# A routed two-layer block on one core: down weights kept in freed memory, powers moved ahead of scatters, tails spread over three engines

## The chip, the cores and the metric

The kernel runs on one core of one Trainium2 chip. The core has five engines that run side by side: TensorE (PE, matrix products), VectorE (DVE), ScalarE (ACT), GpSimd (POOL) and SyncE (SP), which here starts DMAs. The metric is the device time of one execution in microseconds. Of the kernel before, three executions took 945.34, 945.8 and 950.18 us; the median is 945.8 us.

## The reference

The input is x with T = 2048 rows of D = 256 numbers. Four sublayers follow, each on a layer norm of x and added to x:

```
x = x + attn_a(layernorm(x))  # projections q, k, v (causal convolution, 4 taps), gate g; per head a
                              # recurrence: state = rotate(state)*alpha + beta*rotate(v)
                              # out * rsqrt(mean(out^2) + eps) * rms_w * silu(g), then @ Wo
x = x + ffn(layernorm(x))     # 8 experts, top 2 of softmax(h @ router), weights normed:
                              # y = silu(h @ gate) * (h @ up) @ down, summed over both experts
x = x + attn_b(layernorm(x))  # 16 heads of 16, window 128 and 16 persistent keys
x = x + ffn(layernorm(x))     # the same weights as the first ffn
```

The layer norm is (x - mean) / sqrt(var + 1e-5). All arithmetic is float32 in kind.

## The kernel before

Rows lie on the 128 partitions: 16 blocks of 128 tokens, in four groups of four blocks. The program is four stages, one after the other, with a barrier between them.

**Recurrence** (function `recurrence`, the profile's 0 to 277 us). A loop over four chunks of 512 tokens, `it` = 0 to 3. In each, TensorE sums squares per head (L398), VectorE stores them plus eps as `ms` (L713), GpSimd raises them to the power -1/2 (L587), TensorE transposes the result (L408), VectorE splits it (`rms_split`, L718) and scales the output, TensorE projects it back (L428), and VectorE adds it to x and takes statistics (`tail_stats_dve`). `tail_pool` (L154, L156) turns the variance into rstd on GpSimd. During chunk `it` the routing of group `it - 1` is worked out too: logits on TensorE, ranks and slots on VectorE. GpSimd then scatters the group's rows to the DRAM tensor `xs`, sorted by expert: eight indirect DMAs per group (`pool_scatter`, L1096), which wait for the last routing step (`shares`, L1029). On GpSimd's queue the scatters of group `it - 1` stand after `tail_pool` of chunk `it`, and so ahead of the power of chunk `it + 1`.

**Experts** (function `experts`, called twice, L1249 and around). A loop over 39 tiles of 128 sorted rows, in software pipeline steps. SyncE reads each tile from `xs` into `xin` (L1176, ring of four). TensorE transposes it (L1233), multiplies by gate and up (L1249), transposes the hidden values (L1259) and multiplies by the down weights `wd` (L1271). ScalarE copies and scales (L1309, L1316, L1324), VectorE makes products and copies (L1369, L1376) and the target rows (`aim`). GpSimd sends results to `back` in DRAM (L1211), and between them scatters the last group. SyncE issues the reads of the first two tiles, then the read of `wd` (L1193, 2 x 968 KB), then the other tiles. The same queue carries both.

After the tiles comes a tail, four groups of 512 tokens. SyncE reads two blocks of `back` per group, one for each expert (L1187, 512 KB each); two groups fit in memory, so group 2 waits until group 0 has been added. VectorE adds both (`mix`, L1383), takes statistics (L1389, L1393), normalises (L1399) and, after TensorE's transposes (L1282) and ScalarE's copy (L1329), splits off the low part (L1404). GpSimd does the power only. In the second call there is no norm: each group is stored to `out` instead.

**Attention** (function `attention`). Sixteen blocks in software pipeline: period `n` (0 to 19), five steps `u` in each. The tables `LOGITS`, `RANKS`, `RATIOS` and `SEND` name the steps (n, u) at which the routing of groups 0, 1 and 2 and their scatters stand. `max_rows` on SyncE moves the negated row maxima of a block (L1651). `keep` on GpSimd masks the probabilities (L1697, L1699), `rstd_of` does the power of a block's norm (L1688, L1691).

The order on each engine is the order in which the code is written; there is no scheduler. An engine waits at the head of its queue for semaphores.

## Time and profile before

| | us |
|---|---|
| median of three runs | 945.8 |
| the profiled execution | 952.93 |
| its span, first to last instruction | 951.1 |

| engine | busy us | share |
|---|---|---|
| PE, matmuls | 696.6 | 73% |
| DVE | 524.9 | 55% |
| ACT | 285.5 | 30% |
| POOL | 284.7 | 30% |

The mean granted TensorE clock is 0.764 of full speed. Of the 951.1 us the recurrence takes the first 277, the first experts stage runs to 448, attention to 799, the second experts stage to the end. In the profile a bracket after an instruction gives the time that its engine sat idle before it and what ended the wait; idle time counts only where others wait for that engine.

### The profile page before, as it was taken

To read this page: it belongs to the slowest core of one execution; us is meant where nothing else is said; L and a number is where in the kernel's file an instruction comes from. 1 tells how busy PE (TensorE), PEld (TensorE's weight loads), DVE (VectorE), ACT (ScalarE), POOL (GpSimd) and SP (SyncE) were. 2 spreads that over 40 slices of the span, in tenths; PEclk is the share of its full clock that TensorE was granted. 3 is DMA by queue.
4 is the path that set the end of the run, shared out by engine and by line. 5 is a ranking of instruction groups with operands and counts; after the bars stand their busy time and mean duration, and the time that the engine had idled before them with its cause. 6 is when DMAs were issued, how large, how long until landed. Compare 5 with 4: busy or idle time off the path is not lost. (4 is left out here: it accounts for less than half of the span.)

```text
span 951.1 us, 14101 instructions
## 1 busy us (share of the span) xinstructions
PE 696.6 (73%) x4483; PEld 546.2 (57%) x4483; DVE 524.9 (55%) x1373; ACT 285.5 (30%) x518; POOL 284.7 (30%) x345
## 2 busy tenths in 40 slices
PE   2857898866246899912368999998898986689980
PEld 1636676645234577701246787786786764457760
DVE  6493889768533444447444565466656354344434
ACT  1342332331001344401113443433432331224440
POOL 0001111312430544322501333323533553154340
PEclk9887897956565999955556897777965665789995
DMA  7897000100024333251643255145140003333328
GB/s 221 289 351 232 1 1 1 44 4 12 36 67 112 120 112 95 84 178 35 86 56 55 26 68 68 21 50 72 35 73 13 26 19 102 99 111 115 99 84 265
DMA packets 67915, 84.01 MB, mean 88 GB/s; under 512 B 8758, under 2 KB 62659, under 8 KB 67237
## 3 DMA queue, kind: packets, MB, share of 16 engines
q1 hardware_dynamic: 61028, 64.93, 29.3%
q0 software_dynamic: 6816, 18.19, 5.4%
q8 instruction: 39, 0.64, 0.3%
q14 instruction: 32, 0.25, 0.1%
HBM read 32.26 MB, written 39.06 MB: 75 GB/s over the span
## 5 line engine op out<-in xcount | busy, mean ns | idle before, releaser
L1211 POOL DMA_INDIRECT back<-f_yout,f_target x78 | 76.8, 984 | 163.8 <-ACT f_yout L1324 151.7
L1249 PE MATMUL bank<-f_wgu,f_xt 128*128 x312 | 116.0, 497 | 12.5 <-ACT f_xt L1309 10.9
L1369 DVE TENSOR_TENSOR f_hid<-f_act_g,bank 128x176 f32<-128x176 f32 x78 | 26.4, 338 | 126.2 <-ACT f_act_g L1316 101.8
L1249 PEld LDWEIGHTS bank<-f_wgu,f_xt 128*128 128x128 f32 x312 | 60.4, 204 | 42.5 <-issue 21.6
L1096 POOL DMA_INDIRECT xs<-xn,f_slots x64 | 64.5, 1008 | 67.0 <-DVE xn L1029 38.6
L1271 PE MATMUL bank<-f_wd,f_hT 88*128 x312 | 83.5, 392 | 0.0
L1697 POOL TENSOR_SCALAR_AFFINE_SELECT b_prob<-b_prob 128x512 f32<-128x512 f32 x60 | 38.0, 634 | 151.3 <-ACT b_prob L2005 151.2
L2005 ACT ACTIVATE b_prob<-bank 128x1024 f32<-128x1024 f32 x60 | 61.4, 1023 | 57.7 <-PE bank L1823 57.4
L2081 DVE COPY_PREDICATED bank<-b_later,bank 128x512 f32<-128x512 int32 x60 | 41.6, 693 | 49.6 <-PE bank L1794 45.6
L1271 PEld LDWEIGHTS bank<-f_wd,f_hT 88*128 88x128 f32 x312 | 55.4, 198 | 5.0
L1864 PE MATMUL bank<-b_prob,b_V 128*17 128x128 f32 x992 | 47.9, 319 | 12.8 <-POOL b_prob L1699 12.7
L2085 DVE TENSOR_REDUCE b_m<-bank 128x4 f32<-128x512 f32 x64 | 44.3, 692 | 15.7 <-PE bank L1785 13.6
L1699 POOL TENSOR_SCALAR_AFFINE_SELECT b_prob<-b_prob 128x512 f32<-128x512 f32 x64 | 41.3, 646 | 33.4 <-ACT b_prob L2002 33.4
L1324 ACT ACTIVATE f_yout<-bank,f_share 128x256 f32<-128x256 f32 x78 | 36.9, 473 | 43.6 <-issue 22.2
L154 POOL TENSOR_SCALAR vareps<-meanvar 128x4 f32<-128x4 f32 x8 | 5.3, 668 | 142.2 <-DVE meanvar L135 142.2
L1823 PE MATMUL bank<-b_QS,b_KS 64*128 64x128 f32 x496 | 46.2, 308 | 2.3 <-ACT b_prob L2005 1.9
L1823 PEld LDWEIGHTS bank<-b_QS,b_KS 64*128 64x128 f32 x496 | 42.3, 230 | 6.7 <-ACT b_prob L2005 4.3
L1316 ACT ACTIVATE f_act_g<-bank 128x176 f32<-128x176 f32 x78 | 24.7, 317 | 70.5 <-PE bank L1249 67.6
L1309 ACT ACTIVATE f_xt<-bank 128x256 f32<-128x256 f32 x78 | 29.9, 383 | 49.7 <-PE bank L1233 34.6
L1233 PE MATMUL bank<-ident_sb,f_xin 128*128 128x128 f32 x156 | 32.5, 293 | 15.2 <-DMA f_xin<-xs 15.2
L1794 PE MATMUL bank<-b_KS,b_QS 48*128 48x256 f32 x208 | 36.5, 424 | 8.5 <-DVE b_m L2085 5.5
L162 PE MATMUL bank<-ident_sb,xn 128*128 128x128 f32 x64 | 12.4, 357 | 39.2 <-DVE xn L142 39.2
(317 smaller groups left out, 1679.9 us busy)
## 6 DMA issues: line engine op xcount, KB each, us to landing
xs<-f_zero SPq DMA_DIRECT2D x8, 2176.0 KB, 19.7
f_xin<-xs SPq DMA_DIRECT2D x78, 136.0 KB
f_back<-back SPq DMA_DIRECT2D x16, 512.0 KB, 5.0
b_QS<-b_qh SPq DMA_DIRECT2D x32, 128.0 KB
b_KS<-b_kh SPq DMA_DIRECT2D x32, 128.0 KB, 6.0
f_wd<-in_wd SPq DMA_DIRECT2D x4, 968.0 KB
f_wgu<-in_wgu SPq DMA_DIRECT2D x2, 1408.0 KB, 8.3
x_tok<-in_x SPq DMA_DIRECT2D x4, 512.0 KB, 7.3
```

Source lines behind the costliest of these rows:

```text
L1096: pool.indirect_dma_start(m.xs, bass.IndirectOffsetOnAxis(m.slots[:, g, c, i:i + 1], 0), xn[:, g * TPC + i], None)\
L1211: pool.indirect_dma_start(m.back, bass.IndirectOffsetOnAxis(target[:, g % AR:g % AR + 1], 0), yout[:, g % YB], None, bounds_check=2 * 2 * ...
L1249: mm = pe.matmul(psG[:, g % 2, 0:2 * FH], xt[:, g % 2, k * P:(k + 1) * P], m.gu[:, k, bass.ds(e, 2 * FH)], start=k == 0, stop=k == KD - 1)
L1271: mm = pe.matmul(psY[:, g % 2, 0:D], hT[:, g % 2, k * P:(k + 1) * P], wd[:, k, bass.ds(e, D)], start=k == 0, stop=k == 1)
L1324: act.activation(yout[:, g % YB], psY[:, g % 2, 0:D], ACT.Copy, scale=share[:, g % AR:g % AR + 1])\
L1697: pool.affine_select(halves_of[:, :, 0], halves_of[:, :, 0], [[0, 4], [-1, P]], ALU.is_gt, 0.0, base=0, channel_multiplier=1)
L1699: pool.affine_select(halves_of[:, :, 1], halves_of[:, :, 1], [[0, 4], [1, P]], ALU.is_ge, 0.0, base=0, channel_multiplier=-1).then_inc(kep ...
L1823: mm = pe.matmul(own_t[:, half, i, w], KS[rows, 2 * u + i, ring(b - 1 + w)], QS[rows, 2 * u + i, ring(b)], start=True, stop=True)
L1864: mm = pe.matmul(psO[CG * j:CG * j + HV1, u * P:(u + 1) * P], V[:, (b - 1 + w) % RING, 4 * u + j], prob[:, quad(b, u) % 2, half, c:c + P], ...
L2005: ins = act.activation(dst, psT[:], ACT.Exp, scale=SCALE)
L2081: dve.copy_predicated(own_s[:, :, :, 1], later[:].unsqueeze(1).unsqueeze(1).broadcast_to([P, 2, 2, P]), own_s[:, :, :, 0]).then_inc(sel_do ...
L2085: dve.tensor_reduce(mo[:, :, 2 * u:2 * u + 2], own_s[:, :, :, 1], AX.X, ALU.max).then_inc(m_done, 1)
```

## The change

- **Down weights.** `wd` moves out of `experts` into an object that `recurrence` and `attention` open over memory of weights that they have finished with (the right side of SBUF). SyncE reads it with `load_down`: in the recurrence after the last use of the projection weights `wf` and `wv`, in attention in period 15. It is read twice, as before.
- **Powers ahead of scatters.** In the recurrence the scatters of group `it - 2` stand behind the power of chunk `it`; in chunk 3 six of group 2's follow them, ahead of `tail_pool`, and two stand at the end.
- **Tails.** GpSimd adds the first expert's rows (`first_rows`) and works out rstd and rstd times minus mean (`deviation`); VectorE adds the second's (`second_rows`), takes statistics and negates the mean; ScalarE normalises (`unit_norm`). `back` holds all four groups, each half with a semaphore of its own, so all eight reads are issued without a wait.
- **Attention.** The routing of group 2 moves up by two to three steps, its scatters end in period 18, and the tile table moves from (18, 0) to (17, 2).

```diff
@@ recurrence
-        wfh, wfl = sb("wfh", [P, KD, TAPS, 2 * P], F32R), sb("wfl", [P, KD, TAPS, 2 * P], F32R)
-        wvh, wvl = sb("wvh", [P, KD, VT * P], F32R), sb("wvl", [P, KD, VT * P], F32R)
+        with ExitStack() as early:
+            wfh, wfl, wvh, wvl = (early.enter_context(nc.sbuf_tensor(name, shape, F32R, side="right")) for name, shape in (
+                ("wfh", [P, KD, TAPS, 2 * P]), ("wfl", [P, KD, TAPS, 2 * P]), ("wvh", [P, KD, VT * P]), ("wvl", [P, KD, VT * P])))
+        m.open_down(nc, 0)
...
-        SENT_AHEAD = 3
+        SENT_AHEAD = 6
...
                 m.load(sp, t, wfl_done)
+                sp.wait_ge(f_ready, now(NCH - 1))
+                sp.wait_ge(vg_ready, now(NCH - 1, VT, NVG))
+                m.load_down(sp)
...
                     pool.tensor_tensor(rms[:], ms[:], minus_half[:, 0:TPC * HA], ALU.pow).then_inc(rms_ready, 1)
+                    if it > 1:
+                        for i, c in SENDS:
+                            pool_scatter(pool, m, xn, 0, it - 2, i, c)
                     if it == NCH - 1:
                         for i, c in SENDS[:SENT_AHEAD]:
                             pool_scatter(pool, m, xn, 0, it - 1, i, c)
                     tail_pool(pool, tl, it)
-                    if it > 0:
-                        for i, c in SENDS[SENT_AHEAD if it == NCH - 1 else 0:]:
-                            pool_scatter(pool, m, xn, 0, it - 1, i, c)
+                for i, c in SENDS[SENT_AHEAD:]:
+                    pool_scatter(pool, m, xn, 0, NCH - 2, i, c)
@@ Routed
+    def open_down(self, nc, turn):
+        self.wd = self.down.enter_context(nc.sbuf_tensor(f"f_wd{turn}", [FK, 2, NE * 2 * FH], F32, side="right"))
...
+    def load_down(self, sp):
+        for k in range(2):
+            sp.dma_start(self.wd[:, k], self.wd_in_dram[k * FK:(k + 1) * FK]).then_inc(self.d_in, 16)
@@ experts
-        wd = sb("wd", [FK, 2, NE * 2 * FH])
...
-        back = sb("back", [P, 2, 2, TPC, D])
+        back = sb("back", [P, NGRP, 2, TPC, D])
...
-                    if n >= 2:
-                        sp.wait_ge(mix_done, 2 * (n - 1))
...
-                    if s == -1:
-                        for k in range(2):
-                            sp.dma_start(wd[:, k], m.wd_in_dram[k * FK:(k + 1) * FK]).then_inc(d_in, 16)
...
+                def first_rows(g):
+                    pool.wait_ge(back_in[g][0], 16 * (turn + 1))
+                    pool.tensor_tensor(xgrp(g), xgrp(g), back[:, g, 0].rearrange("p b d -> p (b d)"), ALU.add).then_inc(x_new, 1)
+
+                def deviation(g):
+                    pool.wait_ge(mv_done, TPC * (g + 1))
+                    pool.tensor_scalar(vareps[:], mv2[:, g % 2, :, 1], EPS, None, ALU.add).then_inc(ve_done, 1)
...
+                    pool.tensor_tensor(rs2[:, g % 2], vareps[:], minus_half[:, 0:TPC], ALU.pow).then_inc(rstd_done, 1)
+                    pool.wait_ge(rstd_done, g + 1)
+                    pool.tensor_tensor(off2[:, g % 2], rs2[:, g % 2], mv2[:, g % 2, :, 0], ALU.mult).then_inc(off_done, 1)
+
+                for g in range(NGRP):
+                    first_rows(g)
+                    if not last and g > 0:
+                        deviation(g - 1)
...
+                def unit_norm(g):
+                    act.wait_ge(off_done, g + 1)
+                    for i in range(TPC):
+                        act.activation(xn[:, g * TPC + i, 0:D], xgrp(g)[:, i * D:(i + 1) * D], ACT.Identity,
+                                       bias=off2[:, g % 2, i:i + 1], scale=rs2[:, g % 2, i:i + 1]).then_inc(xn_done, 1)
...
+                def second_rows(g):
+                    dve.wait_ge(back_in[g][1], 16 * (turn + 1))
+                    dve.wait_ge(x_new, group_no(turn, g) + 1)
+                    dve.tensor_tensor(xgrp(g), xgrp(g), back[:, g, 1].rearrange("p b d -> p (b d)"), ALU.add).then_inc(mix_done, 1)
@@ attention
-        LOGITS = {(9, 3): 0, (13, 3): 1, (16, 3): 2}
-        RANKS = {(10, 1): 0, (14, 1): 1, (17, 1): 2}
-        RATIOS = {(10, 4): 0, (14, 4): 1, (17, 3): 2}
+        LOGITS = {(9, 3): 0, (13, 3): 1, (16, 1): 2}
+        RANKS = {(10, 1): 0, (14, 1): 1, (16, 3): 2}
+        RATIOS = {(10, 4): 0, (14, 4): 1, (17, 0): 2}
...
-                2: [(17, 4)] + [(n, u) for n in (18, 19) for u in range(NSTEP)][:7]}
+                2: [(n, u) for n in (17, 18) for u in range(1, NSTEP)]}
...
+                    if n == NB - 1:
+                        sp.wait_ge(v_done, NHC)
+                        for hc in (NHC - 2, NHC - 1):
+                            sp.wait_ge(q_in[hc % 2], halves(hc))
+                            sp.wait_ge(k_in[hc % 2], halves(hc))
+                        m.load_down(sp)
```

In the second place, `(n, u) == (18, 0)` for the table on VectorE becomes `(17, 2)`. The attention weights but `bo` and the buffers `lath`, `latl`, `qh`, `ql`, `kh` and `kl` are placed like `wfh` above, with `wd` over them.

Where the order changes, first GpSimd's queue in chunks 1 to 3 of the recurrence, before (L587 is the power of `ms`, L154 and L156 are `tail_pool`):

```order
L587 TENSOR_TENSOR rms<-ms,minus_half 128x24
L154 TENSOR_SCALAR vareps<-meanvar 128x4
L156 TENSOR_TENSOR rstd<-vareps,minus_half 128x4
L1096 DMA xs<-xn,f_slots 16384x272 x8
L587 TENSOR_TENSOR rms<-ms,minus_half 128x24
L154 TENSOR_SCALAR vareps<-meanvar 128x4
L156 TENSOR_TENSOR rstd<-vareps,minus_half 128x4
L1096 DMA xs<-xn,f_slots 16384x272 x8
L587 TENSOR_TENSOR rms<-ms,minus_half 128x24
L1096 DMA xs<-xn,f_slots 16384x272 x3
L154 TENSOR_SCALAR vareps<-meanvar 128x4
```

The same queue and chunks now (L594 is the power, L1113 the scatter):

```order
L594 TENSOR_TENSOR rms<-ms,minus_half 128x24
L154 TENSOR_SCALAR vareps<-meanvar 128x4
L156 TENSOR_TENSOR rstd<-vareps,minus_half 128x4
L594 TENSOR_TENSOR rms<-ms,minus_half 128x24
L1113 DMA xs<-xn,f_slots 16384x272 x8
L154 TENSOR_SCALAR vareps<-meanvar 128x4
L156 TENSOR_TENSOR rstd<-vareps,minus_half 128x4
L594 TENSOR_TENSOR rms<-ms,minus_half 128x24
L1113 DMA xs<-xn,f_slots 16384x272 x14
L154 TENSOR_SCALAR vareps<-meanvar 128x4
L156 TENSOR_TENSOR rstd<-vareps,minus_half 128x4
L1113 DMA xs<-xn,f_slots 16384x272 x2
```

Each power has moved ahead of a run of eight scatters; in the last chunk fourteen now stand between the power and `tail_pool`, where three stood.

SyncE's queue at the start of an experts stage, before (L1172 loads a tile's row number, L1176 reads a tile):

```order
L1176 DMA f_xin<-xs 128x272
L1172 TENSOR_LOAD f_row
L1172 ISA x2
L1176 ISA
L1176 DMA f_xin<-xs 128x272
L1193 DMA f_wd<-in_wd 88x2816 x2
L1172 TENSOR_LOAD f_row
```

And at the end of the recurrence and the start of that stage now (L888 is `load_down`):

```order
L888 DMA f_wd<-in_wd 88x2816 x2
L310 UNCONDITIONAL_BRANCH
L1178 UNCONDITIONAL_BRANCH
L1188 TENSOR_LOAD f_row
L1188 ISA x2
L1192 ISA
L1192 DMA f_xin<-xs 128x272
```

The read of the down weights has left its place between the second and the third tile for the end of the stage before.

VectorE's queue in the tail of the first experts stage, groups 0 and 1, before:

```order
L1383 TENSOR_TENSOR x_tok<-x_tok,f_back 128x1024 x2
L1389 BN_STATS stats<-x_tok 128x6 x4
L1393 BN_AGGR meanvar<-stats 128x2 x4
L1399 TENSOR_SCALAR xn<-x_tok,meanvar,rstd 128x256 x4
L1383 TENSOR_TENSOR x_tok<-x_tok,f_back 128x1024 x2
L1389 BN_STATS stats<-x_tok 128x6 x4
```

And now, for the same groups (L1411 is `second_rows`, L1423 negates the means):

```order
L1411 TENSOR_TENSOR x_tok<-x_tok,f_back 128x1024
L1416 BN_STATS stats<-x_tok 128x6 x4
L1421 BN_AGGR f_mv<-stats 128x2 x4
L1423 TENSOR_SCALAR f_mv<-f_mv 128x4
L1411 TENSOR_TENSOR x_tok<-x_tok,f_back 128x1024
L1416 BN_STATS stats<-x_tok 128x6 x4
```

One add of two and the four normalisations have left VectorE; GpSimd and ScalarE have them.

## Rows read from the trace of the kernel before

**Rows 1.** timeline of GpSimd, 130 to 270 us: start us, us, engine, line, operation, count [idle before]

```profile
243.42 0.96 POOL L1096 DMA_INDIRECT xs<-xn,f_slots  x1 [0.30 <-issue]
244.41 4.20 POOL L587 TENSOR_TENSOR rms<-ms,minus_half 128x24 f32<-128x24 f32 x1
...
268.90 0.23 POOL L154 TENSOR_SCALAR vareps<-meanvar 128x4 f32<-128x4 f32 x1 [4.27 <-DVE meanvar L135]
```

**Rows 2.** timeline of VectorE, 235 to 262 us

```profile
235.36 0.18 DVE L713 TENSOR_SCALAR ms<-bank 128x24 f32<-128x24 f32 x1 [0.55 <-PE bank L398]
...
249.77 0.68 DVE L718 CAST rmsh<-bank 6x512 fp32r<-6x512 f32 x1 [7.49 <-PE bank L408]
...
260.09 0.17 DVE L1029 TENSOR_SCALAR xn<-xn 128x4 f32<-128x4 f32 x1
```

**Rows 3.** timeline of TensorE, 155 to 200 us

```profile
193.84 1.01 PE L408 MATMUL bank<-ident_sb,rms 128*6 128x128 f32 x4 [7.80 <-POOL rms L587]
```

**Rows 4.** timeline of TensorE, 281 to 310 us

```profile
288.90 2.71 PE L1249 MATMUL bank<-f_wgu,f_xt 128*128 x4 [0.56 <-ACT f_xt L1309]
...
305.18 1.35 PE L1249 MATMUL bank<-f_wgu,f_xt 128*128 x4
```

**Rows 5.** timeline of TensorE, 802 to 830 us

```profile
807.42 1.45 PE L1249 MATMUL bank<-f_wgu,f_xt 128*128 x4 [0.56 <-ACT f_xt L1309]
...
823.73 1.40 PE L1249 MATMUL bank<-f_wgu,f_xt 128*128 x4
...
826.27 1.35 PE L1249 MATMUL bank<-f_wgu,f_xt 128*128 x4
```

**Rows 6.** who waited for whom, 281 to 825 us: us in total, times, longest

```profile
PE bank L1233 <- DMA f_xin<-xs: 15.2, 2, 8.3
```

**Rows 7.** busy us by stretch: PE, PEld, DVE, ACT, POOL, then clock, DMA share, GB/s

```profile
292.00:296.00 4.00, 0.14 (x1) 0.00 (x0) 3.36 (x17) 0.00 (x0) 0.00 (x0) 0.50 0.74 166
```

**Rows 8.** timeline of SyncE, 735 to 765 us

```profile
739.91 19.41 SPq L1651 DMA_DIRECT2D b_QS<-b_nmT  x4
```

**Rows 9.** timeline of TensorE, 765 to 770 us

```profile
767.35 1.95 PE L1836 MATMUL bank<-b_QS,b_KPT 128*128 128x128 f32 x8
```

**Rows 10.** timeline of VectorE, 785 to 800 us

```profile
793.23 0.18 DVE L2124 BATCH_NORM_AGGREGATE meanvar<-stats 128x2 f32<-128x6 f32 x1
```

**Rows 11.** timeline of GpSimd, 785 to 800 us

```profile
795.79 0.25 POOL L1688 TENSOR_SCALAR vareps<-meanvar 128x1 f32<-128x1 f32 x1
```

**Rows 12.** timeline of all engines, 777 to 779 us

```profile
777.67 0.64 POOL L1697 TENSOR_SCALAR_AFFINE_SELECT b_prob<-b_prob 128x512 f32<-128x512 f32 x1 [1.54 <-ACT b_prob L2005]
777.74 0.59 DVE L1001 TENSOR_TENSOR f_adj<-f_next,f_cum 128x8 f32<-128x8 f32 x1
778.26 0.64 POOL L1699 TENSOR_SCALAR_AFFINE_SELECT b_prob<-b_prob 128x512 f32<-128x512 f32 x1
...
778.37 0.58 DVE L1002 TENSOR_TENSOR f_slot<-f_pre,f_cum 128x32 f32<-128x32 f32 x1
```

**Rows 13.** costliest groups of the page: busy us, mean ns of one | idle before

```profile
L1697 POOL TENSOR_SCALAR_AFFINE_SELECT b_prob<-b_prob 128x512 f32<-128x512 f32 x60 | 38.0, 634 | 151.3 <-ACT b_prob L2005 151.2
```

**Rows 14.** timeline of VectorE, 410 to 450 us

```profile
414.77 2.48 DVE L1383 TENSOR_TENSOR x_tok<-x_tok,f_back 128x1024 f32<-128x1024 f32 x2 [11.13 <-DMA f_back<-back]
...
436.30 2.48 DVE L1383 TENSOR_TENSOR x_tok<-x_tok,f_back 128x1024 f32<-128x1024 f32 x2
...
440.25 0.38 DVE L1393 BATCH_NORM_AGGREGATE meanvar<-stats 128x2 f32<-128x6 f32 x4
...
446.67 1.23 DVE L1404 TENSOR_TENSOR xTl<-bank,xTh 128x1024 fp32r<-128x1024 f32 x1 [3.12 <-ACT xTh L1329]
```

**Rows 15.** timeline of VectorE, 925 to 951.1 us

```profile
933.40 2.49 DVE L1383 TENSOR_TENSOR x_tok<-x_tok,f_back 128x1024 f32<-128x1024 f32 x2 [11.06 <-DMA f_back<-back]
936.36 2.48 DVE L1383 TENSOR_TENSOR x_tok<-x_tok,f_back 128x1024 f32<-128x1024 f32 x2 [0.48 <-DMA f_back<-back]
...
945.23 2.49 DVE L1383 TENSOR_TENSOR x_tok<-x_tok,f_back 128x1024 f32<-128x1024 f32 x2 [1.43 <-DMA f_back<-back]
```

88 lines of the change are left out of this document (41 added, 47 removed).

## The prediction, made before the result was known

> **What bounds the kernel now.** The engine shares come first: TensorE is busy 73% of the span, VectorE 55%, and no engine is full, so the time is a chain through stages that fill and drain. I then read who waited for whom, stage by stage, and the timelines at the seams. The reader should see four places where a whole chain stands still.
>
> First, the recurrence. In chunk 2 TensorE sits idle for 7.80 us before the transposes of the power [rows 3], and in chunk 3 VectorE waits 7.49 us for the same transposes [rows 2]. On GpSimd the power starts at 244.41, right behind a scatter [rows 1], though its input was ready at 235.36 + 0.18 = 235.54 [rows 2].
>
> Second, the start of both experts stages: TensorE waits twice for the third tile's read, 15.2 us in total [rows 6].
>
> Third, the tail of the first experts stage: from the first add at 414.77 to 446.67 + 1.23 = 447.9 VectorE and one other engine at a time work on four groups, 33.1 us in which no tile is multiplied [rows 14].
>
> Fourth, the ends: the power of the last attention block waits behind scatters [rows 10, 11], and the last four groups are added as their reads arrive [rows 15].
>
> **The change part by part.** The sum is made against the profiled execution, 952.93 us (span 951.1 and 1.8 around it). It is 7.1 us above the median 945.8. All terms are differences, so I take the sum off the median.
>
> *Powers, chunk 2.* The power no longer waits for eight scatters. TensorE's 7.80 us of idleness go [rows 3], and TensorE is then busy with value products until it reaches the transposes, so all 7.8 count. The scatters come behind the power and take 8 x (0.96 + 0.30) = 10.1 us [rows 1], long before this chunk's variance. Term: 7.8.
>
> *Powers, chunk 3.* The power would run from 235.54 for 4.20 us, to 239.8, instead of to 248.6 [rows 1, 2]: 8.9 earlier. But VectorE is busy with comparisons until 249.77 - 7.49 = 242.28, so only its wait of 7.49 is won [rows 2]. Term: 7.5. What is late next: fourteen scatters now stand ahead of `tail_pool`. In before's times less 7.8, the power ends at 232.0, eight scatters at 242.1. The other six wait for `shares`, at 260.26 less 15.3, 245.0 [rows 2], and end at 252.6. The variance that `tail_pool` needs came at 268.90 [rows 1], now 253.6. A margin of 1.0 us covers them; if a scatter costs 0.17 us more, each further tenth costs 0.6.
>
> *Down weights, first stage.* The third tile's read stood behind 1.94 MB of weights, and at 292 to 296 us the DMA engines moved 166 GB/s with nothing else to do [rows 7]: 11.7 us of transfer. Without it the third tile lands before TensorE asks. Tile 1's gate products start at 288.90 and take 2.71 us, the 1.2 GHz level (the granted clock of the stretch behind them is 0.50) [rows 4, 7]. Tile 2 then starts at about 292.9 (2.71 plus two transposes, a copy and their hand-overs). A tile's step is 826.27 - 823.73 = 2.5 us at the upper clock [rows 5] and twice that, 5.0 to 5.3, at the lower. So tile 3 starts at 295.4 to 298.2 instead of 305.18 [rows 4]: 7.0 to 9.8. I take the middle, 8.4: tile 1 still ran at the lower level, but TensorE no longer pauses behind it.
>
> *Down weights, second stage.* Here the clock was already up at tile 1: its gate products start at 807.42 and take 1.45 us. Two steps of 2.5 bring tile 3 to 812.4 instead of 823.73 [rows 5]. Term: 11.3. The twelve small routing steps on VectorE between the second and third tiles lose their cover, about 3 us, and end near 813; the product that waits for them is needed by TensorE only after tile 3's gate products, at 813.6, so nothing is added.
>
> *Where the weights are read now.* In the recurrence the read falls into a stretch in which SyncE has nothing else. In attention it stands in front of the row maxima of block 15. SyncE issues those of block 14 at 739.91, and the run of four ends at 759.32 [rows 8], so the last pair goes out near 758. A load from 741.2 at 166 GB/s ends at 752.9 [rows 7]. The pair is needed at 767.35 [rows 9]. The cost is nothing, with 5 us of cover ahead of the pair and 8 behind it.
>
> *End of attention.* The variance of block 15 is known at 793.23 + 0.18 = 793.41 [rows 10], and the power's first step starts at 795.79 [rows 11]. With the scatters ended a period earlier that is 2.4 us. The scatters instead stand between the maskings of block 15, where GpSimd idles 1.5 us before a masking [rows 12], so a 1.3 us scatter roughly fits. The other moves in the tables I take as nothing, as they bring the same work a few steps sooner. Bounds: 0, if the scatters between the maskings cost what the end wins, and 5, if the earlier steps win as much again. Term: 2.4.
>
> *Tail of the first stage.* One duration is missing: GpSimd adding two tensors of 128 x 1024 from SBUF, R. The nearest row is its masking of 128 x 512 in 0.634 us, one input [rows 13]: 1.27 for 1024 is the lower bound. Its power on 24 columns takes 4.20 us [rows 1], which would be 179 us for 1024; that is the far end. I take two reads per element for one, 2 x 1.27 = 2.5, as the masking is an ordinary elementwise pass and the power is not, and 5.0 as the upper end that I reckon with. By the Trainium skill (GPSIMD Engine Reference, 3.1 Elementwise) an add of 2048 float32 takes 4497 ns; an estimate from it is 2.25 us here, and with 8 adds in chain the sum would be 2.0 us better.
>
> Do the two adds overlap? At 777.67 a masking runs for 0.64 us; VectorE's add of 128 x 8 at 777.74 takes 0.59 and ends at 778.33, as the masking does (778.31); the next one, 0.58, ends with the next masking at 778.9 [rows 12]. So an add with both inputs in SBUF stands still while GpSimd reads SBUF, and I let the adds exclude each other. The Trainium skill says this as a rule (SBUF — State Buffer, SBUF: two separate sides): a VectorE instruction with two SBUF inputs and a GpSimd instruction that reads SBUF take a shared port by exclusive lock. It speaks against this change; by that rule the split wins only what statistics and norms cover, and the trace agrees.
>
> VectorE's add takes 2.48 / 2 = 1.24; from the start of the last pair, 436.30, to the last aggregate, 440.63, are 4.33, of which 1.85 are statistics, 2.05 with the negation [rows 14]. One group then costs 2.5 + 1.24 + 2.05 = 5.8. The first half group lands about 1.5 us before the pair did (halves follow at half of 936.36 - 933.40 [rows 15]), at 413.2. The first means are known at 413.2 + 5.8 = 419.0, the last at 419.0 + 3 x 5.8 = 436.4. Behind the last aggregate came 447.9 - 440.63 = 7.3 us; ScalarE's norm is fed to TensorE block by block, about 1.2 less: 442.5. Term: 5.4. With R = 1.27 VectorE's own 4.5 per group decides (3.3 and the low split of 1.23), and the end is 437.8, 10.1 won. With R = 5.0 a group costs 8.3 and the end is 452.5, 4.6 lost.
>
> *Tail of the last stage.* From 931.9 four groups of 3.74 end at 946.9, against 945.23 + 2.49 = 947.7 [rows 15]. Term: 0.8. With R = 1.27 the last read, at 942.4, decides: 943.6, 4.1 won. With R = 5.0: 956.9, 9.2 lost.
>
> **Sum**: 7.8 + 7.5 + 8.4 + 11.3 + 2.4 + 5.4 + 0.8 = 43.6. The profiled execution would take 909.3; the median 945.8 - 43.6 = 902.2.
>
> **The rivals.**
>
> *A slow add, a GpSimd-bound tail.* R is 5.0: the two tails give 10.0 + 10.0 less, 922.2. For it: no row shows such an add, and the locks are in the trace. Against it: GpSimd's masking runs at near VectorE's rate. Chance 9%.
>
> *The weights were not the cause.* The third tile is late for another reason, say the landing of the scatters: the terms 8.4 and 11.3 stay out, 921.9. For it: both waits are just on tile reads, which share DRAM and queues with everything. Against: the busy DMA share of 0.74 with 166 GB/s fits 1.94 MB [rows 7]. Chance 4%.
>
> *More than forecast.* The adds take 1.3 to 2 us or interleave better, and the clock comes up at once in the first stage: 4.7 + 3.3 + 1.4 = 9.4 more, 892.8. Chance 12%.
>
> *Slower than before.* The eight GpSimd adds are in series on both tails. Each microsecond of R above 2.5 costs 4 in the first tail (one per group) and 4 in the last. The whole gain of 43.6 is eaten at R = 2.5 + 43.6 / 8 = 8.0 us; beyond it the kernel is slower, at R = 9 by 8 x 6.5 - 43.6 = 8.4, 954.2. For it: the power of 24 columns shows how slow GpSimd can be. Against: such a rate is nowhere seen on an ordinary pass. Chance 2%.
>
> **How the numbers follow.** The forecast has 73%. Its own terms vary by about 6 (clock 1.4, attention 2.5, chunk 3's margin 1, R within half a microsecond 4; they seldom add up). The range takes in the faster rival and reaches towards the two near 922: 891 to 915, which leaves out some 18 in 100. About 0.5%, 4.7 us, can be told from no change here. Faster by more than that: 73 + 9 + 4 + 12 = 98, less a little for what I did not see: 0.96. Same: 0.02. Slower: 0.02.
>
> **What would show it.** In the recurrence the power starts within 0.3 us of `ms` in chunks 2 and 3, and `tail_pool` of chunk 3 follows its variance at once; if not, the scatters overran. TensorE's waits for `f_xin` at the third tile are under 1 us, and tile 3 comes 8 us (first stage) and 11 us (second) sooner after the stage's first tile. In the tails GpSimd's adds show R, and VectorE's adds stretch beyond 1.24 where they meet GpSimd's; the first tail takes 29 us from the first landing instead of 33. In attention the last power starts at the variance. The forecast is wrong if R is above 4, if the third tile still waits, or if the transposed maxima of block 15 land behind the weights and TensorE waits at the persistent scores.

## The result, and the profile after

The changed kernel takes 909.9 us at the median of four runs (908.4 to 918.2), the kernel before 948.0 in the runs beside it; the ratio is 0.9605, with a 95% interval of 0.9525 to 0.9685. The profiled execution took 910.46 us with a span of 908.7, against 952.93 and 951.1: 42.4 us of span less, where the steps of the prediction gave 43.6. Between the medians it is 38.1 us.

The recurrence first. This is the timeline of GpSimd in the changed kernel, chunk 3 (it answers to [rows 1]):

```profile
228.66 4.17 POOL L594 TENSOR_TENSOR rms<-ms,minus_half 128x24 f32<-128x24 f32 x1 [14.42 <-DVE ms L722]
...
253.11 0.96 POOL L1113 DMA_INDIRECT xs<-xn,f_slots  x1 [0.30 <-issue]
254.91 0.23 POOL L154 TENSOR_SCALAR vareps<-meanvar 128x4 f32<-128x4 f32 x1 [0.84 <-DVE meanvar L135]
...
257.86 0.96 POOL L1113 DMA_INDIRECT xs<-xn,f_slots  x1 [0.30 <-issue]
```

VectorE beside it ([rows 2]):

```profile
228.41 0.18 DVE L722 TENSOR_SCALAR ms<-bank 128x24 f32<-128x24 f32 x1 [0.55 <-PE bank L405]
...
235.39 0.68 DVE L727 CAST rmsh<-bank 6x512 fp32r<-6x512 f32 x1
...
245.83 0.17 DVE L1046 TENSOR_SCALAR xn<-xn 128x4 f32<-128x4 f32 x1
```

The power starts 0.07 us behind its input and VectorE no longer waits for its transposes. The fourteenth scatter ends at 254.07, and GpSimd then idles 0.84 us for the variance: that is what was left of the margin of 1.0. Chunk 2 is the same: TensorE's transposes of the power, with 7.80 us of idleness ahead of them in [rows 3], have none.

```profile
188.06 1.04 PE L415 MATMUL bank<-ident_sb,rms 128*6 128x128 f32 x4
```

The starts of the two experts stages, TensorE (gate products of tiles 0 to 3; [rows 4] and [rows 5]). First stage, then second:

```profile
268.50 2.71 PE L1272 MATMUL bank<-f_wgu,f_xt 128*128 x4 [0.56 <-ACT f_xt L1332]
...
272.20 2.71 PE L1272 MATMUL bank<-f_wgu,f_xt 128*128 x4 [0.56 <-ACT f_xt L1332]
...
276.42 2.71 PE L1272 MATMUL bank<-f_wgu,f_xt 128*128 x4 [0.56 <-ACT f_xt L1332]
...
281.31 1.35 PE L1272 MATMUL bank<-f_wgu,f_xt 128*128 x4
...
771.71 2.71 PE L1272 MATMUL bank<-f_wgu,f_xt 128*128 x4 [0.56 <-ACT f_xt L1332]
...
775.40 2.71 PE L1272 MATMUL bank<-f_wgu,f_xt 128*128 x4 [0.56 <-ACT f_xt L1332]
...
782.21 1.35 PE L1272 MATMUL bank<-f_wgu,f_xt 128*128 x4
```

No wait for a tile's read is left ([rows 6] had 15.2 us). From tile 0 to tile 3 it was 19.97 us in the first stage and 20.01 in the second, and is now 281.31 - 268.50 = 12.81 and 782.21 - 771.71 = 10.50. The second stage's tile 1 took 1.45 us before and takes 2.71 now: TensorE's clock rose later here.

The tail of the first stage, VectorE ([rows 14]):

```profile
393.25 1.23 DVE L1411 TENSOR_TENSOR x_tok<-x_tok,f_back 128x1024 f32<-128x1024 f32 x1 [12.11 <-POOL x_tok L1230]
...
396.44 0.57 DVE L1423 TENSOR_SCALAR f_mv<-f_mv 128x4 f32<-128x4 f32 x1
...
400.27 1.86 DVE L1423 TENSOR_SCALAR f_mv<-f_mv 128x4 f32<-128x4 f32 x1
...
404.90 2.35 DVE L1411 TENSOR_TENSOR x_tok<-x_tok,f_back 128x1024 f32<-128x1024 f32 x1
...
413.10 0.38 DVE L1421 BATCH_NORM_AGGREGATE f_mv<-stats 128x2 f32<-128x6 f32 x4
413.59 0.17 DVE L1423 TENSOR_SCALAR f_mv<-f_mv 128x4 f32<-128x4 f32 x1
...
419.97 1.22 DVE L1427 TENSOR_TENSOR xTl<-bank,xTh 128x1024 fp32r<-128x1024 f32 x1 [3.12 <-ACT xTh L1358]
```

and GpSimd's adds beside it:

```profile
390.82 2.33 POOL L1230 TENSOR_TENSOR x_tok<-x_tok,f_back 128x1024 f32<-128x1024 f32 x1 [5.58 <-DMA f_back<-back]
...
399.76 2.35 POOL L1230 TENSOR_TENSOR x_tok<-x_tok,f_back 128x1024 f32<-128x1024 f32 x1
...
403.80 2.36 POOL L1230 TENSOR_TENSOR x_tok<-x_tok,f_back 128x1024 f32<-128x1024 f32 x1
```

The missing duration R is 2.34 us. VectorE's add at 404.90 takes 2.35 instead of 1.23: it ends at 407.25, 1.1 us behind the end of GpSimd's add (403.80 + 2.36 = 406.16). The adds exclude each other in this trace. ScalarE's norm of the last group, behind GpSimd's product, is

```profile
415.27 0.20 POOL L1240 TENSOR_TENSOR f_off<-f_rs,f_mv 128x4 f32<-128x4 f32 x1
415.50 2.07 ACT L1353 ACTIVATE xn<-x_tok,f_off,f_rs 128x256 f32<-128x256 f32 x4
```

and VectorE's norm of the same group in the kernel before was

```profile
442.17 1.38 DVE L1399 TENSOR_SCALAR xn<-x_tok,meanvar,rstd 128x256 f32<-128x256 f32 x4 [0.43 <-POOL rstd L1224]
```

From the first reading back to the end of the last low split (VectorE's last step of this tail, the low part of the transposed rows) it is 421.19 - 386.83 = 34.36 us, against 447.90 - 409.32 = 38.58.

The last tail, SyncE, GpSimd and VectorE ([rows 15]):

```profile
886.49 8.09 SPq L1200 DMA_DIRECT2D f_back<-back  x8
890.50 2.33 POOL L1230 TENSOR_TENSOR x_tok<-x_tok,f_back 128x1024 f32<-128x1024 f32 x1 [5.52 <-DMA f_back<-back]
...
900.62 3.36 POOL L1230 TENSOR_TENSOR x_tok<-x_tok,f_back 128x1024 f32<-128x1024 f32 x1 [0.16 <-DMA f_back<-back]
904.09 1.22 DVE L1411 TENSOR_TENSOR x_tok<-x_tok,f_back 128x1024 f32<-128x1024 f32 x1 [2.30 <-POOL x_tok L1230]
```

From the first reading to the end: 908.7 - 886.49 = 22.2 us, against 951.1 - 927.90 = 23.2.

The end of attention ([rows 10, 11]); the variance of block 15 is known at 762.99 and GpSimd takes it up at:

```profile
762.79 0.96 POOL L1113 DMA_INDIRECT xs<-xn,f_slots  x1 [0.31 <-issue]
763.77 0.25 POOL L1720 TENSOR_SCALAR vareps<-meanvar 128x1 f32<-128x1 f32 x1
```

0.8 us late instead of 2.4: three scatters still stand between the last two powers, where five stood.

Where the down weights are read now, in attention, and the two halves of the maxima of block 15 behind them (SyncE; it answers to [rows 8]):

```profile
714.55 1.41 SPq L888 DMA_DIRECT2D f_wd<-in_wd  x2
...
727.43 1.31 SPq L1677 DMA_DIRECT2D b_QS<-b_nmT  x2
```

### The profile page after: what moved, and what is told of

It reads as the page before. It is cut to its first block and busy times, and to the rows that moved or that the text cites. A ratio compares the mean times of both kernels' runs of the same rounds, so it can differ in the third digit from the quotient of the medians.

```text
span 908.7 us, 14109 instructions
## 1 busy us (share of the span) xinstructions
PE 690.4 (76%) x4483; PEld 538.7 (59%) x4483; DVE 516.4 (57%) x1353; ACT 294.0 (32%) x534; POOL 307.2 (34%) x357
## 5 line engine op out<-in xcount | busy, mean ns | idle before, releaser
L1113 POOL DMA_INDIRECT xs<-xn,f_slots x64 | 64.4, 1006 | 31.9 <-issue 13.4
L2118 DVE TENSOR_REDUCE b_m<-bank 128x4 f32<-128x512 f32 x64 | 44.2, 691 | 15.4 <-PE bank L1817 13.4
L154 POOL TENSOR_SCALAR vareps<-meanvar 128x4 f32<-128x4 f32 x8 | 5.3, 667 | 130.6 <-DVE meanvar L135 130.6
L1855 PEld LDWEIGHTS bank<-b_QS,b_KS 64*128 64x128 f32 x496 | 42.4, 231 | 6.7 <-ACT b_prob L2038 4.2
L1332 ACT ACTIVATE f_xt<-bank 128x256 f32<-128x256 f32 x78 | 29.9, 383 | 29.9 <-PE bank L1256 15.2
L1896 PEld LDWEIGHTS bank<-b_prob,b_V 128*17 128x17 f32 x992 | 24.9, 109 | 21.5 <-POOL b_prob L1731 14.4
```

What stands on the lines that cost most here:

```text
L1113: pool.indirect_dma_start(m.xs, bass.IndirectOffsetOnAxis(m.slots[:, g, c, i:i + 1], 0), xn[:, g * TPC + i], None)\
L1855: mm = pe.matmul(own_t[:, half, i, w], KS[rows, 2 * u + i, ring(b - 1 + w)], QS[rows, 2 * u + i, ring(b)], start=True, stop=True)
L1896: mm = pe.matmul(psO[CG * j:CG * j + HV1, u * P:(u + 1) * P], V[:, (b - 1 + w) % RING, 4 * u + j], prob[:, quad(b, u) % 2, half, c:c + P], ...
L2118: dve.tensor_reduce(mo[:, :, 2 * u:2 * u + 2], own_s[:, :, :, 1], AX.X, ALU.max).then_inc(m_done, 1)
```

## The experiments

The times of one kernel scatter by 6 to 19 us from run to run, and the runs below fell on four chips. On three of them an experts stage from its fourth tile to its first reading back takes 96 to 98 us, on the fourth (three scatters ahead, and the filled idle time) 104 to 105, as in the two profiles above. So the experiments are read by the length of each stretch in the profile, one profile for each. How well a stretch repeats is said with it: from the last low split of the recurrence to the first tile's gate products it repeats to 0.01 us, from the means of squares to the add only to about 1 us. The times are medians of all runs; the ratios to the kernel before are those on record, and are not always the quotient of two medians. A stage length given for the changed kernel without a chip is that of its first profile, the one above.

**The scatters ahead of the power again.**

```diff
-        SENT_AHEAD = 6
+        SENT_AHEAD = 3
...
-                    if it > 1:
-                        for i, c in SENDS:
-                            pool_scatter(pool, m, xn, 0, it - 2, i, c)
...
                     tail_pool(pool, tl, it)
-                for i, c in SENDS[SENT_AHEAD:]:
-                    pool_scatter(pool, m, xn, 0, NCH - 2, i, c)
+                    if it > 0:
+                        for i, c in SENDS[SENT_AHEAD if it == NCH - 1 else 0:]:
+                            pool_scatter(pool, m, xn, 0, it - 1, i, c)
```

> The changed kernel with the order on GpSimd in the recurrence as it was before the change: the scatters of a chunk stand ahead of the next chunk's power again. Theory (the power's place was worth the two waits it removes): what the trace of the changed kernel shows from the means of squares to the add of the chunk is given back, 7.9 us in chunk 2 and 7.0 in chunk 3, 14.9 in all, so about 909.9 + 14.9 = 924.8, ratio about 1.016. Rival (the recurrence was also helped by the two weights' reads leaving the start of the experts, or the stage after absorbs part of it, since the first experts tile waits for routing steps anyway): the difference is under 12 or over 18 us, and the logits of the first experts stage do not move with the add of chunk 3.

Measured: 913.1 us at the median, 0.972 of the kernel before (0.962 to 0.982). From the start of the means of squares to the start of the add it takes 35.29 us in chunk 2 (changed kernel 27.44) and 30.37 in chunk 3 (23.33): 7.9 and 7.0 given back. Over all twelve profiles with the new order of powers the two stretches are 26.6 to 27.4 and 22.1 to 23.3, which makes it 7.8 to 8.7 and 7.0 to 8.3. TensorE's wait is there again:

```profile
193.54 1.02 PE L415 MATMUL bank<-ident_sb,rms 128*6 128x128 f32 x4 [7.76 <-POOL rms L594]
```

So the theory holds for the recurrence. But a part of the rival came true as well, for the logits did not move with the add: between the last low split, VectorE's last step in the recurrence, and tile 0 of the experts it is 8.85 us, as before the change, and 6.14 in the changed kernel. That is 2.7 us which no term of the forecast had, and 17.6 in all.

**Three scatters ahead instead of six**, the powers in their new place:

```diff
-        SENT_AHEAD = 6
+        SENT_AHEAD = 3
```

> The changed kernel with three instead of six scatters of chunk 2 ahead of the variance steps of chunk 3; the powers keep their new place, five scatters instead of two stand behind those steps. The forecast took the recurrence's gain from the powers alone; the traces show 2.7 us more between the last low split of the recurrence and the first tile of the experts (8.85 us in the kernel before and with the old order, 6.14 in the changed kernel). Theory A (the stage ends for all engines with GpSimd's last scatter, and the change left two there instead of five): the means of squares to the add stay at 27 and 22 to 23 us, and the low split to the first gate products takes 8.85 us again, 2.7 us more. Theory B (that stretch is set by the powers' order or by the landing of the scatters of chunks 1 and 2, which now go out earlier): it stays at 6.1.

Measured (one run, 915.0 us): the means to the add stay at 27.4 and 23.3 us, and the low split to tile 0 takes 8.86. The end of the stage, from the timelines of GpSimd, VectorE and TensorE:

```profile
260.24 0.96 POOL L1113 DMA_INDIRECT xs<-xn,f_slots  x1 [0.30 <-issue]
```

```profile
259.73 1.22 DVE L147 TENSOR_TENSOR xTl<-bank,xTh 128x1024 fp32r<-128x1024 f32 x1 [3.18 <-ACT xTh L167]
```

```profile
265.16 0.35 PE L954 MATMUL bank<-f_wr,xTh 128*128 128x16 f32 x1 [6.52 <-PEq L176]
```

The logits start 3.96 us behind the last scatter (261.20) and 4.2 behind the low split (260.95). In the kernel before it is 3.95 behind the scatter, in the experiment above 3.95. In the ten other profiles with the changed kernel's order on GpSimd and nothing on TensorE behind its transposes, it is 1.48 to 1.50 us behind the low split, and 4.1 to 5.0 behind the scatter. So the logits come with the later of the two, low split + 1.49 or last scatter + 3.95, and having three more scatters ahead of the variance was worth 2.7 us at this seam besides. Theory A holds. Whether it is the scatter's own end that counts or the landing of its data, the profile, which has no landing times for it, can't say.

**The down weights read in each stage again.**

```diff
                 for s in range(-3, STEPS):
+                    if s == -1:
+                        m.load_down(sp)
                     if 0 <= s + 3 < G:
```

(and the two other places of `load_down` taken out)

> The changed kernel with the down weights read in each experts stage again, behind the read of the second tile; the buffers stay where the change put them. Theory (only the place of the third tile's read behind 1.94 MB mattered): tile 3 of the first stage comes 7.2 us later and tile 3 of the second 9.5 us later, 16.7 in all, about 926.6, ratio 1.018. Reading of the forecast's own terms: 8.4 + 11.3 = 19.7, about 929.6. Rival (the third tile was late for the landing of the scatters, not for the weights): under 5 us. Rival on the clock: if the read of the weights is what brought TensorE's upper level at tile 1 of the second stage (1.45 us for its gate products before the change, 2.71 after), tile 1 takes 1.45 us here; if it is how TensorE ends the attention stage, it still takes 2.71.

Measured: 915.4 us at the median of four runs that lie 18.5 us apart (902.4 to 920.9), 0.984 of the kernel before (0.975 to 0.994); in the profile, which is of the shortest of the four, TensorE waits again before the third tile of either stage:

```profile
280.19 0.69 PE L1255 MATMUL bank<-ident_sb,f_xin 128*128 128x128 f32 x2 [6.84 <-DMA f_xin<-xs]
...
776.44 0.69 PE L1255 MATMUL bank<-ident_sb,f_xin 128*128 128x128 f32 x2 [6.70 <-DMA f_xin<-xs]
```

Tile 0 to tile 3 takes 19.76 and 18.98 us. The twelve profiles without the read there say what that is to be compared with, and it is not one number: 12.2 to 13.0 us when tiles 0 to 2 run at the lower clock level, 10.5 when tile 2 has the upper one, 8.7 to 8.8 when tile 1 has it too. The read costs 6.8 to 11.0 us in the first stage and 6.0 to 10.3 in the second. Against the changed kernel's most frequent values (10.5 in the first stage, 8.7 to 8.8 in the second, each in six of the twelve) it is 9.3 + 10.3 = 19.6, the forecast's 19.7; against its first profile 7.0 + 8.5 = 15.4. The rival, scatters that land late, is out: nothing else was moved. The clock's rival is out too: tile 1 of the second stage takes 2.71 us here, with the read, and in half of the profiles without it, so the read does not decide that level.

**The tails as before, with all reads at once.**

```diff
-                for g in range(NGRP):
-                    first_rows(g)
...
+                    for e in range(2):
+                        dve.wait_ge(back_in[g][e], 16 * (turn + 1))
+                    for e in range(2):
+                        dve.tensor_tensor(xgrp(g), xgrp(g), back[:, g, e]..., ALU.add)
...
+                def unit_norm(g):      # on VectorE, as before the change
```

> The changed kernel with the arithmetic of both tails as it was before the change: VectorE waits for both halves of a group, does both adds and the norm, GpSimd only the power. All eight reads still go out at once into buffers of their own. Theory A (the split over three engines is what won): the first tail gives back 4.2 us and the last 1.0, about 915.1, ratio 1.006. Theory B (reading all rows at once is what won in the last tail, and the split cost something there, since an add of GpSimd takes 2.33 us and shuts out VectorE's): the last tail does not get slower, it ends 1 to 3 us earlier, and the first gives back 1 to 4 us; between 908 and 913.

Measured: 890.8 us, 0.954 of the kernel before (0.946 to 0.962), not to be told from the changed kernel's ratios (0.949 on two later chips, 0.9605 on the first). The first tail takes 37.74 us where the profiles with the changed kernel's first tail have 34.0 to 35.0: 2.7 to 3.7 given back. The last ends 20.5 us after its first reading, where the split has 21.6 to 22.8: 1.1 to 2.3 faster without the split. VectorE's last pair in this kernel, which waits half a microsecond for its rows and is otherwise back to back:

```profile
884.76 2.48 DVE L1400 TENSOR_TENSOR x_tok<-x_tok,f_back 128x1024 f32<-128x1024 f32 x2 [0.48 <-DMA f_back<-back]
```

Theory B holds. The forecast's 0.8 for the last tail, measured as 1.0, is the sum of two larger things: reads that no longer wait for a buffer (23.2 to 20.5, 2.7 won) and adds in series on two engines (1.7 lost, 22.2 against 20.5, and 1.1 in those profiles of the split that issue their reads as fast as this one).

**Both adds on VectorE, each half as it lands.**

```diff
+                def first_rows(g):
+                    dve.wait_ge(back_in[g][0], 16 * (turn + 1))
+                    dve.tensor_tensor(xgrp(g), xgrp(g), back[:, g, 0]..., ALU.add).then_inc(x_new, 1)
```

(and GpSimd's `first_rows` taken out)

> The changed kernel with both adds of a group on VectorE, each as its half arrives; the norm stays on ScalarE, power and product on GpSimd. Theory A (GpSimd's adds are what costs in the tails: 2.33 us each, in which VectorE's adds and its negation stand still): a group costs VectorE 1.23 + 1.23 + 1.95 = 4.4 us and one low split of 1.22 more from the second group on, the last aggregate comes 1 to 2 us earlier than in the changed kernel, and the last tail ends with its last read, 1.5 to 2.5 us earlier; together 3 to 4 us faster, ratio to the changed kernel 0.996. Theory B (the split of the adds is what made the first tail faster): the first tail gives back its 4 us, and the kernel is 2 us or more slower than the changed one.

Measured: 887.4 us, 0.952 (0.946 to 0.958), beside 883.0 and 0.949 of the changed kernel on the same chip: the whole time shows nothing of the 3 to 4 us that theory A promised. The last tail is what theory A said: its last add ends 15.8 us after the first reading (changed kernel 17.9 to 19.0) and the program 20.3 after it. The first tail takes 34.83 us (changed kernel on that chip 34.15), neither the 1 to 2 us less of A nor the 4 more of B. Three rows of VectorE show why: the aggregates of the second group end at 386.74, and then it waits for the first group's transposes, because the low split stands ahead of the third group's adds in its order. Behind the split those adds wait for no read.

```profile
386.84 0.17 DVE L1420 TENSOR_SCALAR f_mv<-f_mv 128x4 f32<-128x4 f32 x1
390.01 1.23 DVE L1424 TENSOR_TENSOR xTl<-bank,xTh 128x1024 fp32r<-128x1024 f32 x1 [2.99 <-ACT xTh L1351]
391.15 1.22 DVE L1403 TENSOR_TENSOR x_tok<-x_tok,f_back 128x1024 f32<-128x1024 f32 x1
```

In the first tail GpSimd's adds are thus as good as VectorE's own, no better, while in the last tail of these two profiles they cost 1.3 us of the program's end (21.6 against 20.3).

**The negation on GpSimd.**

```diff
                     pool.tensor_scalar(vareps[:], mv2[:, g % 2, :, 1], EPS, None, ALU.add)...
+                    pool.tensor_scalar(mv2[:, g % 2, :, 0], mv2[:, g % 2, :, 0], -1.0, None, ALU.mult)...
```

> The changed kernel with the negation of the means on GpSimd, right behind the add of epsilon and ahead of the power, instead of on VectorE. In the changed kernel this VectorE step of 0.17 us took 0.57 and 1.86 us in the second and first groups, where GpSimd added. Theory A (it stands still with GpSimd's add, although it reads a single tensor of SBUF, and the whole group behind it is late): the last aggregate of the first tail comes 1.5 to 2.5 us earlier. Theory B (the wait only moves: VectorE's next add meets GpSimd's next add instead): under 0.7 us. In both the last tail stays as it is, 18 to 19 us.

Measured: 893.9 us, 0.961 (0.953 to 0.968); the first tail takes 33.96 us, 0.2 less than the changed kernel's on that chip. The stretched steps are gone from VectorE, but GpSimd's negation of the first group took 1.14 us beside VectorE's add, and VectorE now idles 3.47 us ahead of its first low split, where the changed kernel has a stretched negation of 1.86 us and then 1.62 us of idleness; the add behind it meets GpSimd's as before:

```profile
389.22 1.22 DVE L1427 TENSOR_TENSOR xTl<-bank,xTh 128x1024 fp32r<-128x1024 f32 x1 [3.47 <-ACT xTh L1360]
390.36 2.52 DVE L1413 TENSOR_TENSOR x_tok<-x_tok,f_back 128x1024 f32<-128x1024 f32 x1
```

Theory B: the wait only moves.

**GpSimd's add done twice.**

```diff
+                    pool.wait_ge(spared, group_no(turn, g))
+                    pool.tensor_tensor(spare[:], xgrp(g), back[:, g, 0]..., ALU.add).then_inc(spared, 1)
```

> The changed kernel with every add of GpSimd in the tails done twice, the first time into a tile that nobody reads: the cost R of an add goes from 2.33 to 4.67 us. It prices the forecast's rule that each microsecond of R costs 4 us in the first tail and 4 in the last. Theory A (that rule): 4 x 2.33 = 9.3 us more in either tail, 18.7 in all. Theory B (the changed kernel's tails have slack, as its reads arrive every 3 to 4 us and VectorE's statistics lie beside GpSimd's adds): the last tail 4.67 x 4 from its first landing, 6 to 7 us more, the first 7 to 9 us more, 13 to 16 in all. Rival (adds of GpSimd lie wholly beside VectorE's work): under 8 us.

Measured: 901.2 us, 0.965 (0.959 to 0.972). The first tail takes 39.24 us, 5.1 more than the 34.15 of the changed kernel on that chip, the last one 30.1 to the end against 21.6, 8.5 more; 13.6 in all for 2.33 us of R, or 2.2 and 3.6 us per microsecond where the forecast's rule says 4 and 4. The last tail shows the exclusion from both sides:

```profile
888.12 2.33 POOL L1232 TENSOR_TENSOR f_spare<-x_tok,f_back 128x1024 f32<-128x1024 f32 x1
888.26 3.27 DVE L1414 TENSOR_TENSOR x_tok<-x_tok,f_back 128x1024 f32<-128x1024 f32 x1 [14.32 <-POOL x_tok L1233]
890.41 3.32 POOL L1233 TENSOR_TENSOR x_tok<-x_tok,f_back 128x1024 f32<-128x1024 f32 x1
```

VectorE's add started 0.14 us behind GpSimd's and ended 1.1 us behind its end; GpSimd's next add then stood for 1 us behind VectorE's. The forecast's rule is right to a tenth in the last tail and nearly twice too dear in the first, where the second addition lies beside VectorE's statistics, aggregates and negation. The sum of 13.6 us is theory B's 13 to 16, but its parts are not: it had 6 to 7 for the last tail and 7 to 9 for the first.

**The tables of attention as before.**

```diff
-        LOGITS = {(9, 3): 0, (13, 3): 1, (16, 1): 2}
+        LOGITS = {(9, 3): 0, (13, 3): 1, (16, 3): 2}
...
-                2: [(n, u) for n in (17, 18) for u in range(1, NSTEP)]}
+                2: [(17, 4)] + [(n, u) for n in (18, 19) for u in range(NSTEP)][:7]}
```

(and the other three likewise)

> The changed kernel with the five tables of attention (logits, ranks, shares, scatters, expert table) as they were before the change; the down weights are still read there at block 15's maxima. Theory A (the power of the last block behind fewer scatters is all that was won, the forecast's term): 2.4 us given back, of which the trace of the changed kernel shows 1.6, about 912. Theory B (the attention stage from its first read to the logits was 5.3 us shorter in the changed kernel, and all of it comes from the tables): 5.3 given back, about 915.2, ratio 1.006. Rival: the stage was shorter for a reason outside the tables; then the time stays within 1 us of 909.9. On the clock: if the end of attention decides whether TensorE has its upper level at tile 1 of the second experts stage, the gate products there take 1.45 us here instead of 2.71, and up to 1.3 us of the loss is hidden.

Measured: 889.0 us, 0.953 (0.947 to 0.960). VectorE's last aggregate and the norm that waits for the power:

```profile
746.12 0.18 DVE L2157 BATCH_NORM_AGGREGATE meanvar<-stats 128x2 f32<-128x6 f32 x1
749.63 0.41 DVE L2163 TENSOR_SCALAR xn<-x_tok,meanvar,rstd 128x256 f32<-128x256 f32 x1 [3.33 <-POOL rstd L1723]
```

3.51 us from the one to the other, 3.50 in the kernel before, 1.9 in the changed kernel's first profile and 1.19 in its two others, where the last of the three scatters ends before the variance is known. So the tables are worth 1.6 to 2.3 us there. The rest of the stage, from the end of the first tail to that aggregate, takes 340.1 us with the old tables here, 345.3 in the kernel before, 341.6 in the changed kernel's first profile, and 336.5 to 352.5 in all profiles with the new ones: the 3.7 us by which it was shorter in that first profile can't be given to them. Theory A. TensorE's tile 1 of the second experts stage took 2.71 us here and 1.45 in the kernel before, with the same tables.

**The changed kernel again, twice**, on two other chips.

> The changed kernel itself, beside the experiments of this call, since the first four experiments ran on another chip than the kernel before and the changed one did (there the kernel before took 938.5 us at the median, not 948.0, and each experts stage from its fourth tile to its first reading back took 96 us instead of 105). Theory (that difference belongs to the chip, not to the edits): the changed kernel is here as much faster than the kernel before as it was there, ratio 0.95 to 0.965, and its experts stages take 96 us if the chip is of the second kind. By stage I expect from the means of squares to the add 27.4 us in chunk 2 and 23.3 in chunk 3, 10.5 or 12.9 us from tile 0 to tile 3 of the first experts stage (which of the two by when TensorE's clock rises), 34 to 35 us from the first reading back to the end of the first tail, 18 to 19 in the last.

> The changed kernel itself again, on the same chip as the version it is compared with. Ratio to the kernel before 0.945 to 0.965, by which chip it is; last tail 18 to 19 us to the last add and 21.6 to 22.4 to the end; logits 1.49 us behind the last low split of the recurrence.

Measured: 883.0 us, 0.9487 of the kernel before (0.943 to 0.955), and 887.4, 0.9485 (0.943 to 0.954). Stage by stage the first has 34.15 us for the first tail, 21.6 for the last, 10.50 and 8.73 for tiles 0 to 3; the second 34.05, 21.7, 12.81 and 8.71. From the means of squares to the add the second has the 27.4 and 23.3 us expected, the first 27.0 and 22.4, and its ratio is just below the range given. Both took 96 us from the fourth tile to the first reading back, in either experts stage. The difference from the first chip lies there in the main. In the first profile TensorE stands for 3.59 us ahead of its gate products at 306.37 and VectorE for 3.54 us beside it; TensorE waits for ScalarE there, and ScalarE and VectorE for nothing that the profile names. The granted clock goes from 1.00 to 0.50 behind it, and back. Each of the eight experts stages that take 104 to 106 us has one such pause of 3.6 to 4.0 us, the two of the kernel before among them (3.56 us at 330.13), and none of the twenty that take 96 to 98 has one. So it goes with the chip and is no part of the comparison; what makes it, no run shows.

Beside these two ratios, the whole time sets apart only three of the edits so far: the scatters ahead of the power, the weights in the stage, and the add done twice.

**TensorE's idle time filled** with products that nobody reads.

```diff
+                fill(44)
                 tail_pe(pe, tl, NCH - 1)
+                fill(20)
```

(and 6, 12 and 8 around the last steps of attention)

> The changed kernel with products that nobody reads in TensorE's idle time: 44 of 128 x 256 ahead of the last transposes of the recurrence and 20 behind them, and 6, 12 and 8 around the end of attention. In every run so far the logits and the first gate products of both experts stages ran at the lower clock level (2.71 us for tile 0), with TensorE idle for some 10 us just ahead of them, and tile 1 or 2 at either. Theory A (the clock falls in that idle time and rises after TensorE has been busy again for a while): with the gaps filled the first stage begins at the upper level, the 16 logits products take 1.8 us instead of 3.5, tile 0 1.35 to 1.45 us, and from the last low split to tile 3 it is 4 to 6 us less; in the second stage, where TensorE's clock is down for some 40 us ahead of the end of attention, 2 to 4 us less. About 0.7% faster than the changed kernel. Theory B (the level follows something other than TensorE's own recent work): tile 0 stays at 2.71 us, and the fillers cost 0 to 4 us where they delay the transposes.

Measured: 910.7 us, 0.957 (0.951 to 0.963) on a chip where the kernel before takes 950. The clock by stretch (busy time of PE, PEld, VectorE, ScalarE, GpSimd, then the granted clock):

```profile
252.00:258.00 6.00, 4.88 (x42) 4.68 (x41) 3.95 (x13) 0.00 (x0) 4.34 (x6) 1.00 0.19 73
258.00:262.00 4.00, 3.10 (x27) 2.90 (x25) 1.22 (x1) 1.03 (x1) 0.41 (x1) 1.00 0.14 44
262.00:268.00 6.00, 3.96 (x18) 3.72 (x18) 0.33 (x2) 0.00 (x0) 0.00 (x0) 0.63 0.16 46
```

The products kept TensorE at 2.4 GHz to the end of the recurrence (its last transposes took 1.09 us instead of 1.94, and the low split came 0.9 us sooner), but they also ended last: TensorE reached the stage's end at 261.1 and the logits started 2.95 us later, 3.0 behind the low split and no longer 1.49. In that pause the clock went to 1.2 GHz (granted 1.00 from 262 to 263, 0.79 from 263 to 264, 0.50 from 264 on); tile 0 took 2.71 us. Neither theory as stated: with work put into TensorE's idle time the upper level lasted some 10 us longer than in the changed kernel's first profile (to 263.6 instead of 253.8), and the pause between the stages, in which TensorE has no instruction, was enough in this profile to lose it. In the second stage nothing was won.

**What the experiments point to.**

```diff
-                    second_rows(g)
+                    if last:
+                        both_rows(g)       # both adds on VectorE
+                    else:
+                        second_rows(g)
```

(and 40 filling products ahead of the last transposes of the recurrence)

> The changed kernel with what the experiments point to: in the last tail alone both adds of a group stand on VectorE, each as its half arrives (the first tail keeps GpSimd's adds), and 40 products that nobody reads fill TensorE's idle time ahead of the last transposes of the recurrence, with none behind them. By stage: the last tail ends its adds 15.8 us after its first reading back instead of 17.9 to 19.0, and the program ends 20.3 us after it instead of 21.6 to 22.4, 1.3 to 2 us less; the last low split of the recurrence comes 0.9 us sooner after the add, and the logits 1.49 us behind it. Together 2 to 3 us faster than the changed kernel, which the times of whole runs may not tell apart, as they scatter by more. Rival: reads and stores of the last tail share the DMA engines, so that its end is set by 6.3 MB and not by the adds; then the program ends as late as in the changed kernel, 21.6 us or more after the first reading.

Measured: 884.8 us, 0.947 of the kernel before (0.942 to 0.952), beside 887.4 and 0.9485 of the changed kernel on the same chip: 2.6 us at the median, and not told apart. The recurrence gave its 0.9 us. The last tail did not: the last add ended 17.4 us after the first reading, not 15.8, and the program 22.2, which by the recorded text is the rival's outcome (21.6 or more). The third of the eight reads came late,

```profile
875.48 1.22 DVE L1415 TENSOR_TENSOR x_tok<-x_tok,f_back 128x1024 f32<-128x1024 f32 x1 [2.15 <-DMA f_back<-back]
```

and SyncE took 8.8 us to issue the eight, where it took 7.2 in the kernel with both adds on VectorE everywhere. The changed kernel's last tail follows that issue too: it ends 21.6 to 21.7 us after the first reading in the profiles where the issue took 7.1 to 7.6 us, and 22.1 to 22.8 where it took 8.1 to 8.5. The DMA engines carry 330 to 390 GB/s through most of this tail. So with both adds on VectorE the end was once 20.3 and once 22.2, and how much of the tail belongs to the reads and how much to the adds stays open.

## Why the prediction was right, step by step

**The sum and its base.** The steps gave 43.6 us and the span lost 42.4. For the profiled execution the text said 909.3, and it was 910.46. That this came out so near is in part luck. The seven stretches that the text priced gave 7.9 + 7.0 + 7.2 + 9.5 + 1.6 + 4.2 + 1.0 = 38.4 us, 5.2 less than forecast, most of it in the down weights and the first tail. What made up for it was not in the text: 2.7 us at the seam behind the recurrence and 3.7 in the rest of attention, which is scatter; the other stretches lost 2.4. The terms for the powers, the weights and the first tail stand on experiments that undo them; the end of attention and the last tail came near in size with a step wrong in each, as told below.

The time of 902.2 lay 7.7 under the median of 909.9. Of this 2.2 are the base, since a fourth run of the kernel before brought 945.8 to 948.0. The other 5.5 are the gain, 38.1 between the medians: the sum was worked out from an execution of 952.93, 4.9 above that median, and then taken off the median. On the two chips of the later runs the gain between the medians was 44 to 51 us (931.5 to 887.4 and 933.9 to 883.0).

**Powers.** 7.8 and 7.5 forecast; 7.9 and 7.0 measured, and the same again by undoing it, with about 1 us of scatter in the stretches compared. In chunk 3 the comparisons did run through, and what was late next was named rightly (the margin of the fourteen scatters, 0.84 left of 1.0). What was left out is the seam behind: the text costed the scatters ahead of the variance as a risk and did not see that those behind it hold up the end of the stage. It is 2.7 us, more than any single term was off by.

**Down weights.** 8.4 and 11.3 forecast; 7.2 and 9.5 in the first profile. The mechanism is shown by putting the read back. The size is a matter of when TensorE's clock rises, as the text said for the first stage (7.0 to 9.8; the profiles have 7.0 to 7.5, 9.5 and 11.2) and did not say for the second: it took tile 1 at the upper level because the one profile of before had it so. In seven of fourteen profiles it has, and there the term is 11.3; in this one it had not.

**Where the weights are read now.** No cost: no wait of TensorE for a DMA shows behind it. The load was issued at 714.6, which in before's times (26.7 us later) is the 741.2 of the text, and the maxima of block 15 went out as a pair at 727.4, 3.9 us ahead of where the text had them. A cost of a few microseconds within the scatter of that stage is not excluded: from the end of the first tail to the last aggregate it takes 345.3 and 336.5 us in the two profiles without the load (the kernel before, and the weights read in the stage) and 340 to 352 in the twelve with it. No run isolates it.

**End of attention.** 2.4 forecast, 1.6 in the first profile, 2.3 in two others. The text took it that no scatter would stand ahead of the last power any more; three do, and whether they are done when the variance comes decides between the two numbers. A further 3.7 us of the stage is scatter, by the profile with the old tables.

**Tail of the first stage.** 5.4 forecast, 4.2 measured. R was taken as 2.5 and is 2.34; a group was to cost 5.8 and costs 5.7 (from the first aggregates at 396.33 to the last at 413.48, three groups). The last means were to be known 27.1 us after the first reading and were, after 26.9. The step that was off is the last: behind the last means the end was to come 1.2 us sooner than before (6.1), as ScalarE's norm is fed to TensorE block by block; it came 7.4 behind the last means, and 7.3 behind the last aggregate before the change. The norm takes ScalarE 2.07 us for four blocks where VectorE took 1.38, and a product of 0.20 us on GpSimd stands ahead of it. One bound in this part does not follow from its own terms, though nothing hangs on it: for R = 1.27 it is 413.2 + 4 x 4.5 + 6.1 = 437.3 and not 437.8.

The estimate of 2.25 us from the Trainium skill (GPSIMD Engine Reference, 3.1 Elementwise) was nearer to 2.34 than the 2.5 that was used. The Trainium skill's rule on the shared port (SBUF — State Buffer, SBUF: two separate sides) agrees with the add of 2.35 us at 404.90. The rule has a second half that the prediction left out: a VectorE step with a single input also takes the port if it runs in a mode that uses both ports. The Trainium skill names tensor_scalar as one that can (SBUF — State Buffer, Who interferes with whom). The trace agrees: the negation of 0.17 us took 1.86 beside GpSimd's add, and four bn_stats steps took 1.40 us with an add of GpSimd beside them (at 394.52) and 1.40 without one (at 411.67). The experiment with the negation elsewhere won nothing by avoiding it.

**Tail of the last stage.** 0.8 forecast, 1.0 measured, right by two errors that cancel: the reads that no longer wait for a buffer were worth 2.7, which the text did not price by itself, and the split cost 1.1 to 1.7.

**The rivals.** A slow add is out by R = 2.34. That the weights were not the cause is out. The slower rival's rule of 8 us for each microsecond of R measured 5.8 between R = 2.33 and 4.67; an estimate from that puts its turning point at 2.3 + 43.6 / 5.8 = 9.8 and not at 8.0. More than forecast came true in part on the other chips: tiles 0 to 3 take up to 4 us less there than in the first profile, as the clock rises sooner. The kernel before has no profile on those chips, so where the rest of their 44 to 51 us lies stays open.

## What to carry to other kernels

Ask of every instruction that is moved not only what it delays but which end of a stage it stands in front of: here the last scatter in GpSimd's queue held up TensorE at the barrier, though the logits that TensorE computes next do not use it. When an add is split between VectorE and GpSimd, count both in series, and count the engine whose steps lie between them; where nothing but the adds stands between the reads and the end, as in the last tail, the second engine won nothing in any profile. And price a stage's start at both levels of TensorE's clock, since one profile shows but one of them.

## What was not expected of the hardware

Behind the end of the recurrence TensorE started the experts 1.49 us after VectorE's last step or 3.95 us after GpSimd's last scatter, whichever was later, to 0.02 us in thirteen profiles; the other stage ends do not follow these two numbers (behind the first tail TensorE starts 7.18 us after VectorE's last step, in all fourteen). The first gate products of an experts stage ran at the lower level in all 28 stages, with TensorE kept busy up to 3 us before the stage's first products or not; tile 1 had the upper level in 9 of them and tile 2 in 16, with no edit that decided it. Between chips the changed kernel differs by 2 to 3%. The middles of its two experts stages have 18 us of it, out of the 21 and 29 us of span by which the first profile exceeds the two others, with the pause of 3.6 us in each of them on the slower chip only.
